# The last group's residual add, moved from VectorE into an accumulating scatter

## The chip, the cores and the metric

The kernel runs on one core of a Trainium2 chip. The metric is the device time of one execution in microseconds (us); several executions are timed and their median counts.

## What is computed

There are 2048 tokens of width 512 (x is 4 x 512 x 512). The first half adds to x the product of one of four experts, chosen by the token's id; an expert's gate, up and down weights are all the same 512 x 512 matrix, a slice of ctx. The second half adds a gated feed-forward product with 512 x 1536 weights that are rounded to eight-bit floats. Cut to what matters:

```python
x = x + tanh(g_xattn[0]) * experts(layernorm(x), token_ids, ctx)
gate = silu(layernorm(x) @ q(gate_w) * gate_scale)
up = layernorm(x) @ q(up_w) * up_scale
x = x + tanh(g_ffn[0]) * ((gate * up) @ q(down_w) * down_scale)
```

The last sum is the one that the change is about: x after the experts (x1 below), plus the scaled feed-forward product.

## The kernel before, in words

The tokens are sorted by expert. `order` holds, for each of 16 tiles of 128 sorted tokens, the row of x (and of the output) that each token has. GpSimd gathers the rows of x into `xs` (128 partitions, 16 tiles, 512 values) by an indirect DMA for each tile (L427). Nineteen expert steps (16 tiles and 3 places where a tile has two experts, `STEPS`) then add the expert's product into `xs` on VectorE (`add_expert`, L936, semaphore `x1_done`). After the last of them `xs` holds x1. Beside the steps GpSimd rounds the 36 weight slabs (`round_slab`, L481 and L484), and goes on with the late ones when the steps are over.

The feed-forward half goes over 4 groups of 4 tiles (`GROUPS`, `TPG`). For each group TensorE works through 12 units of the inner dimension: gate and up products (L1322), then the down product of a unit (`down_tile`, L1329), accumulated for the group's four tiles in the PSUM banks `ACC`. When a tile's accumulation ends, VectorE multiplies it by `dsb` (the down scale times tanh of g_ffn) into `slab_tile(g, t)`, which lies in the place of the group's transposed input `X2`, no longer needed, and signals `acc_free` (L1139). 

Who adds this to x1 depends on the group. For groups 0 to 2 GpSimd does: it waits for `acc_free`, adds into `xs` (L525), waits for its own `added`, and scatters the tile's rows to the output by an indirect DMA (L531). For group 3, the last, VectorE itself adds, right after the tile's scaling (L1142, semaphore `added_last`), and GpSimd only issues the scatter. GpSimd executes its queue in the order written: weight rounding, then tiles 0 to 15, then a wait for all 16 scatters (`stored`), after which the kernel ends.

TensorE's order at the very end is written out by hand: for tiles 0 to 2 of the last group the accumulations end first, each with its own signal, then comes the whole rest of tile 3 (its last three units, six matmuls).

Of the kernel before, what the change touches and what calls it, by code (L numbers as in the profile page):

```python
# [17 lines left out]
ALU = mybir.AluOpType  # L18
# [15 lines left out]
def build(nc, x, token_ids, ctx, g_xattn, g_ffn, gate_w, up_w, down_w, gate_scale, up_scale, down_scale, out):  # L34
    B, S, D = x.shape
    TOK = B * S
    TILES = TOK // P
# [4 lines left out]
    STEPS = TILES + E - 1  # L42
    GROUPS = TOK // 512
    TPG = TILES // GROUPS
# [12 lines left out]
    out_rows = out.rearrange("b s d -> (b s) d")  # L57
# [6 lines left out]
    with ExitStack() as stack:  # L64
        def sb(name, shape, dt):
            return stack.enter_context(nc.sbuf_tensor(name, shape, dt))

        def sem(name):
            return stack.enter_context(nc.semaphore(name))


        xs = sb("xs", [P, TILES, D], F32)
# [54 lines left out]
        order = sb("order", [P, TILES], I32)  # L127
# [114 lines left out]
        x1_done = sem("x1_done")  # L242
# [25 lines left out]
        acc_done = sem("acc_done")  # L268
        acc_free = sem("acc_free")
        added = sem("added")  # L270
        added_last = sem("added_last")
        stored = sem("stored")

        N_CONSTS = 14
# [1 line left out]
        def slab_tile(g, t):  # L276

            v = X2[:, g, :, :, :, :] if isinstance(g, int) else X2[:, ds(g, 1), :, :, :, :]
            pat = "p a k t i -> p (a k t i)" if isinstance(g, int) else "p g a k t i -> p (g a k t i)"
            return v.rearrange(pat).bitcast(F32)[:, t * D:(t + 1) * D]  # L280
# [112 lines left out]
        def _(pool):  # L393
            g = nc.gpsimd
# [124 lines left out]
                round_slab(n, slab_slot(n))  # L519


            for t in range(TILES):
                if t < TILES - TPG:
                    pool.wait_ge(acc_free, TPG + t + 1)
                    g.tensor_tensor(xs[:, t, :], xs[:, t, :], slab_tile(t // TPG, t % TPG),  # L525
                                    ALU.add).then_inc(added, 1)
                    pool.wait_ge(added, t + 1)
                else:

                    pool.wait_ge(added_last, t - (TILES - TPG) + 1)  # L530
                g.indirect_dma_start(out=out_rows[:], out_offset=bass.IndirectOffsetOnAxis(  # L531
                    ap=order[:, t:t + 1], axis=0), in_=xs[:, t, :], in_offset=None).then_inc(stored, 16)
            pool.wait_ge(stored, 16 * TILES)


# [207 lines left out]
        def _(dve):  # L743
            v = nc.vector
# [196 lines left out]
            def ffn_norms(norms, a0, a1):  # L941

                if a0 == 0:
                    dve.wait_ge(scales_done, 1)
                    dve.wait_ge(norm_done, EARLY_NORMS)
                    v.tensor_copy(late_norms[:, 0:2 * KC], SMALL[:, 4 * KC * KC:4 * KC * KC + 2 * KC])
                for a in range(a0, a1):

                    src = norms[:, (a - a0) * 2 * KC * KC:(a - a0 + 1) * 2 * KC * KC]
                    ins = v.tensor_reduce(col_ssq[:, :, a * KC:(a + 1) * KC],  # L950
                                          src.rearrange("p (w k j) -> p w j k", w=2, k=KC), AX.X, ALU.add)
                link(ins, norms_read, nread)
                c = slice(a0 * KC, a1 * KC)
                v.tensor_tensor(nn[:, c], col_ssq[:, 0, c], col_ssq[:, 1, c], ALU.mult)
                link(v.tensor_tensor(gu[:, c], gs[:, c], us[:, c], ALU.mult), fchain, fcount)
                link(v.tensor_tensor(gu2[:, c], gu[:, c], gu[:, c], ALU.mult), fchain, fcount)
                link(v.tensor_tensor(b2[:, c], nn[:, c], gu2[:, c], ALU.mult), fchain, fcount)
                v.tensor_scalar(b2c[:, c], b2[:, c], 1e-30, 1e38, ALU.max, ALU.min).then_inc(b2_done, 1)

            def ffn_scales(i, a0, a1):  # L960

                c = slice(a0 * KC, a1 * KC)
                dve.wait_ge(binv_done, i + 1)
                link(v.tensor_scalar(f_scale[:, c].bitcast(I32), f_top[:, c].bitcast(I32), POW2_MASK, None,
                                     ALU.bitwise_and), fchain, fcount)
                v.tensor_scalar(gate_mul[:, c], gs[:, c], 1.0 / X_SCALE, None, ALU.mult)
                link(v.tensor_scalar(up_mul0[:, c], us[:, c], 1.0 / X_SCALE, None, ALU.mult), fchain, fcount)
                v.tensor_tensor(up_mul[:, c], up_mul0[:, c], f_scale[:, c], ALU.mult)
                v.reciprocal(f_inv[:, c], f_scale[:, c]).then_inc(fscale_done, 1)
# [98 lines left out]
            last = v.value_load(walk_last[0:1, 0:1], min_val=0, max_val=4095)  # L1068
# [6 lines left out]
            def late_slabs(c):  # L1075

                for n in range(EARLY + 2 * c, min(EARLY + 2 * c + 2, SLABS)):
                    slab_big(n, slab_slot(n))

            def late_norm(c):  # L1080

                dve.wait_ge(norm_done, EARLY_NORMS + 2 * (c - 4))
                v.tensor_copy(late_norms[:, 2 * KC * (c - 4):2 * KC * (c - 3)],
                              GATE[(c + 1) % 2][:, 0:2 * KC]).then_inc(norm_read, 1)

            def unit_fuse(g, c):
                u = g * IC + c
                dve.wait_ge(up_done, u + 1)
                dve.wait_ge(sg_done, u + 1)
                if not (isinstance(g, int) and g * IC + c < 2):  # L1090
                    dve.wait_ge(fl_done, u - 1)
                v.scalar_tensor_tensor(out=fuse[:, c % 2, :], in0=UP[c % 2][:], scalar=up_mul[:, c:c + 1],  # L1092
                                       in1=sg[:, c % 2, :], op0=ALU.mult, op1=ALU.mult).then_inc(fuse_done, 1)

            def unit_low(g, c):
                u = g * IC + c
                if not (isinstance(g, int) and g * IC + c < 2 or is_last_unit(g, c)):
                    dve.wait_ge(down_done, u - 1)
                dve.wait_ge(fh_done, u + 1)  # L1099
                v.tensor_tensor(fuse_part(g, c, 1), fuse[:, c % 2, :], fuse_part(g, c, 0),  # L1100
                                ALU.subtract).then_inc(fl_done, 1)
# [16 lines left out]
            def group(g, first, last):  # L1118
                for c in range(2, IC):
                    unit_fuse(g, c)  # L1120
                    if first and 5 <= c < 8:
                        late_norm(c)
                    unit_low(g, c)
                    if first:
                        late_slabs(c)
                    if first and c == 7:
                        dve.wait_ge(norm_read, 3)
                        ffn_norms(late_norms, 2, 3)
                        ffn_scales(1, 2, 3)
                if not last:  # L1130
                    unit_fuse(g + 1, 0)
                    unit_low(g + 1, 0)

                for t in range(TPG):
                    if t < TPG - 1 or last:
                        dve.wait_ge(acc_done, g * (TPG - 1) + t + 1)
                    else:
                        dve.wait_ge(down_done, g * IC + IC)
                    v.tensor_tensor(slab_tile(g, t), ACC[t][:], dsb[:], ALU.mult).then_inc(acc_free, 1)  # L1139
                    if last:  # L1140
                        dve.wait_ge(acc_free, TPG + g * TPG + t + 1)
                        v.tensor_tensor(xs[:, g * TPG + t, :], xs[:, g * TPG + t, :], slab_tile(g, t),  # L1142
                                        ALU.add).then_inc(added_last, 1)
                if not last:
                    unit_fuse(g + 1, 1)
                    unit_low(g + 1, 1)

            group(0, True, False)
            with dve.Fori(1, GROUPS - 1) as gi:
                group(gi, False, False)  # L1150
            group(GROUPS - 1, False, True)


# [259 lines left out]
```

## Time and profile before

| | |
|---|---|
| Time, median of 3 runs | 439.34 us (437.16 to 439.57) |
| Profiled execution, its own time | 434.8 us |
| Its span, first to last instruction | 433.1 us |
| Busy: TensorE | 394.0 us |
| Busy: VectorE | 230.8 us |
| Busy: ScalarE | 188.7 us |
| Busy: GpSimd | 172.1 us |
| Scatter issue (L531), median of 16 | 983 ns |

In the rows below the engines are PE (TensorE matmuls), PEld (TensorE weight loads), DVE (VectorE), ACT (ScalarE), POOL (GpSimd) and SP (the queue that loads). A row of a timeline gives the start and the duration in us, engine, line, operation, what is written <- what is read, and in brackets how long the engine had been idle and who ended that. The program's names stand without their buffer numbers, so X is X2. A row of busy times gives the stretch and its length, the busy time (and number of instructions) of PE, PEld, DVE, ACT and POOL, the granted TensorE clock as a share of full speed, the busy share of the 16 DMA engines, and GB/s. An indirect DMA's row on POOL is the issue alone; its data moves later, and its landing is when its semaphore is complete.

### The profile page before, as it was taken

Reading aid. Unit: us, or ns where it says so; the run is one execution under the profiler, and the core shown is the slowest. Engines: PE = TensorE matmul, PEld = TensorE weight load, DVE = VectorE, ACT = ScalarE, POOL = GpSimd, SP = SyncE. Lnnn points to the kernel's source line nnn. Section 1 sums busy time; section 2 is a strip of 40 time slices with the busy share of each in tenths; the row PEclk is TensorE's granted clock in tenths of the full one; section 3 lists DMA queues with packets and bytes.
Section 4 is the critical chain, followed back from the end, with each engine's and each line's share of the span. In section 5 each row is a group of like instructions: output and inputs, shape, how many; then the busy total and the mean of one; then the engine's idle time right before and its main releaser. Section 6 shows DMA issues by size and latency. Waiting matters only on the chain. (4 is left out here: it accounts for less than half of the span.)

```text
span 433.1 us, 6969 instructions
## 1 busy us (share of the span) xinstructions
PE 394.0 (91%) x2012; PEld 197.4 (46%) x2013; DVE 230.8 (53%) x479; ACT 188.7 (44%) x305; POOL 172.1 (40%) x209
## 2 busy tenths in 40 slices
PE   3288989899989999899989999999999999999991
PEld 3245545465546555344434444444444444444440
DVE  5668888777776679558642423223522224232234
ACT  4456656776776664765352222222222222222220
POOL 3445489635595547789640520000800001700003
PEclk9769999999999999899999999999999999999996
DMA  6583411110122121222000110000100000200002
GB/s 208 185 289 103 119 49 30 51 43 24 50 73 51 39 82 50 65 82 90 10 0 0 51 48 2 0 0 2 73 24 0 0 0 0 97 2 1 2 0 97
DMA packets 10507, 22.64 MB, mean 52 GB/s; under 512 B 1624, under 2 KB 1648, under 8 KB 10480
## 3 DMA queue, kind: packets, MB, share of 16 engines
q1 hardware_dynamic: 7920, 13.92, 10.7%
q0 software_dynamic: 2560, 8.39, 5.6%
q8 instruction: 13, 0.21, 0.2%
q14 instruction: 14, 0.11, 0.1%
HBM read 18.11 MB, written 4.19 MB: 51 GB/s over the span
## 5 line engine op out<-in xcount | busy, mean ns | idle before, releaser
L1322 PE MATMUL bank<-X,W 128*128 128x512 f16 (+1 forms) x768 | 174.6, 381 | 0.0
L1322 PEld LDWEIGHTS bank<-X,W 128*128 128x128 bf16 x768 | 75.5, 98 | 90.8 <-issue 1.6
L1092 DVE SCALAR_TENSOR_TENSOR cs<-bank,up_mul,cs 128x512 f32<-128x512 f32 x48 | 36.0, 750 | 112.7 <-PE bank L1322 107.2
L1329 PE MATMUL bank<-W,cs 128*128 128x512 bf16 x376 | 88.7, 379 | 2.0 <-DVE cs L1100 2.0
L681 ACT ACTIVATE cs<-bank,gate_mul 128x512 f32<-128x512 f32 x48 | 32.9, 686 | 81.7 <-PE bank L1322 79.3
L525 POOL TENSOR_TENSOR xs<-xs,X 128x512 f32<-128x512 f32 x12 | 15.3, 1273 | 123.9 <-DVE X L1139 123.7
L688 ACT ACTIVATE cs<-cs 128x512 f16<-128x512 f32 x47 | 29.5, 628 | 76.5 <-DVE cs L1092 75.5
L1329 PEld LDWEIGHTS bank<-W,cs 128*128 128x128 f16 x376 | 36.5, 98 | 45.9 <-DVE cs L1100 2.5
L1100 DVE TENSOR_TENSOR cs<-cs 128x512 f16<-128x512 f32 x47 | 34.5, 734 | 36.8 <-ACT cs L688 34.4
L481 POOL TENSOR_TENSOR w_sum<-ws,w_big 128x512 f32<-128x512 f32 x36 | 47.2, 1311 | 5.5 <-DVE w_big L887 3.5
L484 POOL TENSOR_TENSOR W<-w_sum,w_big 128x512 bf16<-128x512 f32 (+1 forms) x36 | 46.4, 1290 | 3.4 <-POOL w_sum L481 1.1
L531 POOL DMA_INDIRECT out<-xs,order x16 | 16.7, 1045 | 50.9 <-DVE xs L1142 47.5
L435 POOL TENSOR_TENSOR ln_tab<-prep,ln_half 128x1 f32<-128x1 f32 (+2 forms) x25 | 16.7, 668 | 46.9 <-DVE prep L785 46.7
L1230 PE MATMUL bank<-Mh,xTh 128*128 x76 | 29.8, 393 | 2.7 <-DVE xTl L907 1.6
L1230 PE MATMUL bank<-Ml,xTh 128*128 x76 | 29.8, 392 | 0.0
L1230 PE MATMUL bank<-Mh,xTl 128*128 x76 | 29.6, 390 | 0.0
L1230 PE MATMUL bank<-Mh,hTh 128*128 x76 | 28.8, 379 | 0.0
L1230 PE MATMUL bank<-Ml,hTh 128*128 x76 | 28.8, 379 | 0.0
L1230 PE MATMUL bank<-Mh,hTl 128*128 x76 | 28.8, 379 | 0.0
L887 DVE TENSOR_SCALAR w_big<-w_big 128x512 f32<-128x512 f32 x36 | 25.7, 738 | 1.5 <-ACT w_big L585 1.4
L585 ACT ACTIVATE w_big<-ws 128x512 f32<-128x512 f32 x36 | 21.3, 618 | 6.3 <-DMA ws<-in_L_ffn_up_w 3.4
L1183 PE MATMUL bank<-ident,cs 128*128 128x128 f32 x64 | 10.7, 323 | 11.3 <-DVE Ml L881 8.5
(148 smaller groups left out, 430.4 us busy)
## 6 DMA issues: line engine op xcount, KB each, us to landing
cs<-in_ctx SPq DMA_DIRECT2D x4, 1024.0 KB, 5.6
ws<-in_L_ffn_gate_w SPq DMA_DIRECT2D x12, 256.0 KB, 2.6
ws<-in_L_ffn_up_w SPq DMA_DIRECT2D x12, 256.0 KB, 2.6
ws<-in_L_ffn_down_w SPq DMA_DIRECT2D x12, 256.0 KB, 2.6
dsc<-in_L_ffn_down_scale SPq DMA_DIRECT2D x1, 256.0 KB
xs<-in_x,order POOLq DMA_INDIRECT x16, 3.7
out<-xs,order POOLq DMA_INDIRECT x16, 2.8
ids<-in_itok_BxS SPq DMA_DIRECT2D x1, 8.0 KB, 1.6
```

Source lines behind the costliest of these rows:

```text
L435: g.tensor_tensor(ln_tab[:, rr, lo:hi, 0], prep[:, slot:slot + 1, lo:hi, 1], ln_half[:, :, lo:hi], ALU.pow).then_inc(ln_chain, 1)
L481: g.tensor_tensor(w_sum[:], ws[:, slot], w_big[:, slot], ALU.add).then_inc(sum_done, 1)
L484: g.tensor_tensor(dst, w_sum[:], w_big[:, slot], ALU.subtract).then_inc(q_done, 1)
L585: a.activation(w_big[:, slot], ws[:, slot], ACT.Abs, scale=FP8_STEP).then_inc(abs_done, 1)
L681: a.activation(sg[:, c % 2, :], GATE[c % 2][:], ACT.Silu, scale=gate_mul[:, c:c + 1]).then_inc(sg_done, 1)
L688: a.activation(fuse_part(g, c, 0), fuse[:, c % 2, :], ACT.Copy).then_inc(fh_done, 1)
L887: v.tensor_scalar(w_big[:, slot], w_big[:, slot], FP8_FLOOR, None, ALU.max).then_inc(big_done, 1)
L1092: v.scalar_tensor_tensor(out=fuse[:, c % 2, :], in0=UP[c % 2][:], scalar=up_mul[:, c:c + 1], in1=sg[:, c % 2, :], op0=ALU.mult, op1=ALU.mu ...
L1100: v.tensor_tensor(fuse_part(g, c, 1), fuse[:, c % 2, :], fuse_part(g, c, 0), ALU.subtract).then_inc(fl_done, 1)
L1230: ins = t_.matmul(dst[:], lhs[:, k * P:(k + 1) * P], rhs, start=(n == 0), stop=(n == 3 * KC - 1))
L1322: ins = t_.matmul(dst[c % 2][:], w, x2_group(g, part, k), start=(k == 0 and part == 0), stop=(k == KC - 1 and part == 1))
L1329: ins = t_.matmul(ACC[t][:], fuse_part(g, c, part)[:, t * P:(t + 1) * P], W8[:, down_slab(c), :], start=(c == 0 and part == 0), stop=(c == ...
```

## The change

The last group's tiles (12 to 15) are written to the output twice. First, as soon as all expert steps are done and GpSimd has finished rounding weights, plain scatters write their x1 rows (semaphore `stored_x1`). At the end, VectorE only scales; GpSimd waits for `acc_free` and issues a scatter of the scaled product itself, with an addition to what lies in the output rows (`compute_op=ALU.add`). Ahead of these stands a wait until the first four scatters have landed. Groups 0 to 2 are as before.

```diff
@@ -519,17 +519,23 @@
-            for t in range(TILES):
-                if t < TILES - TPG:
-                    pool.wait_ge(acc_free, TPG + t + 1)
-                    g.tensor_tensor(xs[:, t, :], xs[:, t, :], slab_tile(t // TPG, t % TPG),
-                                    ALU.add).then_inc(added, 1)
-                    pool.wait_ge(added, t + 1)
-                else:
-
-                    pool.wait_ge(added_last, t - (TILES - TPG) + 1)
+            def scatter(t, rows, op, done):
                 g.indirect_dma_start(out=out_rows[:], out_offset=bass.IndirectOffsetOnAxis(
-                    ap=order[:, t:t + 1], axis=0), in_=xs[:, t, :], in_offset=None).then_inc(stored, 16)
+                    ap=order[:, t:t + 1], axis=0), in_=rows, in_offset=None, compute_op=op).then_inc(done, 16)
+
+            pool.wait_ge(x1_done, STEPS)
+            for t in range(TILES - TPG, TILES):
+                scatter(t, xs[:, t, :], ALU.bypass, stored_x1)
+            for t in range(TILES - TPG):
+                pool.wait_ge(acc_free, TPG + t + 1)
+                g.tensor_tensor(xs[:, t, :], xs[:, t, :], slab_tile(t // TPG, t % TPG),
+                                ALU.add).then_inc(added, 1)
+                pool.wait_ge(added, t + 1)
+                scatter(t, xs[:, t, :], ALU.bypass, stored)
+            pool.wait_ge(stored_x1, 16 * TPG)
+            for t in range(TILES - TPG, TILES):
+                pool.wait_ge(acc_free, TPG + t + 1)
+                scatter(t, slab_tile(t // TPG, t % TPG), ALU.add, stored)
             pool.wait_ge(stored, 16 * TILES)
@@ -1137,10 +1143,6 @@
                     v.tensor_tensor(slab_tile(g, t), ACC[t][:], dsb[:], ALU.mult).then_inc(acc_free, 1)
-                    if last:
-                        dve.wait_ge(acc_free, TPG + g * TPG + t + 1)
-                        v.tensor_tensor(xs[:, g * TPG + t, :], xs[:, g * TPG + t, :], slab_tile(g, t),
-                                        ALU.add).then_inc(added_last, 1)
```

## Rows read from the trace of the kernel before

**Rows 1.** The page, busy us (share of the span) of each engine.

```profile
PE 394.0 (91%) x2012; PEld 197.4 (46%) x2013; DVE 230.8 (53%) x479; ACT 188.7 (44%) x305; POOL 172.1 (40%) x209
```

**Rows 2.** The chain of waits, its end: start us, us, what.

```profile
418.51 3.04 PE bank L1329 x14
421.54 0.02 issue
421.57 0.70 DVE X L1139
422.29 0.69 DVE xs L1142
...
426.27 0.70 DVE xs L1142
426.98 0.27 issue
427.24 0.96 POOL out L531
```

**Rows 3.** Timeline of the end, VectorE, TensorE and GpSimd.

```profile
421.57 0.69 DVE L1139 TENSOR_TENSOR X<-bank,dsb 128x512 f32<-128x512 f32 x1 [0.88 <-PE bank L1329]
...
423.09 0.59 PE L1329 MATMUL bank<-W,w_sum 128*128 128x512 bf16 x2
423.26 0.96 POOL L531 DMA_INDIRECT out<-xs,order  x1 [46.43 <-DVE xs L1142]
...
424.59 0.96 POOL L531 DMA_INDIRECT out<-xs,order  x1 [0.37 <-DVE xs L1142]
...
427.24 0.96 POOL L531 DMA_INDIRECT out<-xs,order  x1 [0.37 <-DVE xs L1142]
```

**Rows 4.** Busy time by quarter microsecond, from 428.50 on.

```profile
428.50:428.75 0.25, 0.00 (x0) 0.00 (x0) 0.00 (x0) 0.00 (x0) 0.00 (x0) 0.50 0.00 0
428.75:429.00 0.25, 0.00 (x0) 0.00 (x0) 0.00 (x0) 0.00 (x0) 0.00 (x0) 0.50 0.96 377
429.00:429.25 0.25, 0.00 (x0) 0.00 (x0) 0.00 (x0) 0.00 (x0) 0.00 (x0) 0.50 0.98 377
429.25:429.50 0.25, 0.00 (x0) 0.00 (x0) 0.00 (x0) 0.00 (x0) 0.00 (x0) 0.50 0.77 295
429.50:429.75 0.25, 0.00 (x0) 0.00 (x0) 0.00 (x0) 0.00 (x0) 0.00 (x0) 0.50 0.02 0
```

**Rows 5.** Scatters (L531): ns min/median/max of the issue; last issue's landing.

```profile
L531 POOL DMA_INDIRECT out<-xs,order x16: 958/983/1153, 243.4 to 427.2; - x16
...
DMA to landing us min/median/max: 2.7/2.7/2.7
```

**Rows 6.** Timeline of VectorE, the last expert step's addition.

```profile
172.65 0.73 DVE L936 SCALAR_TENSOR_TENSOR xs<-bank,y_scale,xs 128x512 f32 x1
```

**Rows 7.** Timeline of GpSimd around its idle time from 221 us.

```profile
220.11 1.27 POOL L484 TENSOR_TENSOR W<-w_sum,w_big 128x512 bf16<-128x512 f32 x1
241.86 1.27 POOL L525 TENSOR_TENSOR xs<-xs,X 128x512 f32<-128x512 f32 x1 [20.49 <-DVE X L1139]
```

**Rows 8.** Busy time in two stretches of 5 us.

```profile
220.00:225.00 5.00, 3.01 (x15) 1.23 (x14) 2.19 (x3) 3.29 (x6) 1.30 (x2) 1.00 0.00 0
225.00:230.00 5.00, 5.00 (x25) 2.29 (x24) 1.45 (x3) 1.92 (x3) 0.00 (x0) 1.00 0.00 0
```

**Rows 9.** Timeline of GpSimd, two of the gathers issued back to back.

```profile
43.89 0.94 POOL L427 DMA_INDIRECT xs<-in_x,order  x1 [0.30 <-issue]
45.14 0.95 POOL L427 DMA_INDIRECT xs<-in_x,order  x1 [0.31 <-issue]
```

**Rows 10.** The page's DMA issues: gathers, then scatters, us to landing.

```profile
xs<-in_x,order POOLq DMA_INDIRECT x16, 3.7
out<-xs,order POOLq DMA_INDIRECT x16, 2.8
```

More of the change, by code:

```diff
@@ L270, in build @@
         added = sem("added")
-        added_last = sem("added_last")
+        stored_x1 = sem("stored_x1")
         stored = sem("stored")
```

## The prediction

> **What bounds the kernel now.** I read the page's busy shares first, then the end of the chain of waits, then the last 12 us in order of time, then the DMA share in quarter microseconds. The first view says that TensorE sets the span: it is busy for 394.0 of 433.1 us, and VectorE and GpSimd for about half of it or less [rows 1]. The change touches TensorE nowhere, so at most the stretch after TensorE's last needed result can move. The chain shows that stretch: TensorE is on it until 421.54; from 421.57 VectorE alternates a scaling and an addition four times, until 426.97; then comes one scatter issue on GpSimd from 427.24 [rows 2]. So the chain's tail is eight VectorE operations of 0.69 us and one issue. The timeline shows what the chain doesn't name: GpSimd issues all four scatters of the last group in that stretch, 0.96 us each, starting at 423.26, 424.59, 425.92 (this one not shown) and 427.24, that is 1.33 us apart, each 0.3 to 0.4 us after its addition; TensorE's very last matmuls end at 423.68 [rows 3]. GpSimd is therefore nearly as full as VectorE here, which matters below. The windows show what follows an issue: for the last one (427.24) the DMA engines are idle until 428.75, work at 0.96 to 0.98 share until 429.5, and are done [rows 4]. Its landing is 2.7 us after the issue [rows 5], at 429.94. The span ends 3.16 us later, with nothing busy; the change leaves that end as it is.
>
> I write the landing of a scatter as: issue start + 1.5 us to the first data, 0.7 us of burst (0.96 + 0.98 + 0.77 of a quarter microsecond each is 0.68), 0.5 us to the semaphore.
>
> **Part 1: the early scatters of x.** Four more indirect scatters go on GpSimd's queue, behind the last weight rounding and ahead of the first addition of group 0, with a wait on the last expert step. The wait costs nothing: the last addition of an expert's product into xs is at 172.65 [rows 6], and GpSimd only comes free at 220.11 + 1.27 = 221.38 [rows 7]. The four issues take 4 x 1.25 = 5.0 us (the spacing comes from the row in part 2), until about 226.4. What is queued behind them is the addition of tile 0, which before started at 241.86 after 20.49 us of idling [rows 7]; so they lie in idle time with 15 us to spare. Without that cover they would move group 0's additions and scatters by up to 5.0 us, and even that would reach no other engine: only GpSimd's own scatters follow from these additions. The transfers (1 MB more written) find an empty DMA side: 0 GB/s from 220 to 230 [rows 8]. No queue of SP or ACT is passed. The second new wait, for these four scatters to have landed, stands ahead of the last group's scatters; with issue by 226 and landing 3 us on it has been met for some 190 us. Cost: 0.
>
> **Part 2: VectorE's additions go, GpSimd gets the chain.** The four additions (0.69 us each, 2.8 us) leave VectorE. Its first scaling still ends at 422.26. The second and third follow at once and end at 422.95 and 423.65; the fourth waits for TensorE's end at 423.68 and ends near 424.4. That is 2.6 us earlier than the 426.97 of before. But it isn't the gain, because the issues now stand end to end. The first can start 0.28 us after the first scaling, at 422.54. The nearest row for back-to-back indirect issues is the row of gathers, one after another with no wait between: 43.89, 45.14, so 1.25 us apart (0.94 busy and 0.31 of issue) [rows 9]. The fourth then starts at 422.54 + 3 x 1.25 = 426.29 instead of 427.24. All four scalings are ready before their issue (424.4 + 0.28 against 426.29), so GpSimd alone sets the pace, and 0.95 us is all that can be saved if an accumulating scatter costs what a plain one costs. Nothing excludes this end of the range, but nothing goes below it: the accumulating form does all the plain one does.
>
> **Part 3: the price of accumulating.** No row of before shows an accumulating transfer. It has two prices.
>
> The burst b. A plain burst keeps the 16 engines at a share of 0.96 to 0.98 for its whole length [rows 4], so it is limited by the engines' work, not by latency. The accumulating one must read the rows of the product and the rows in the output, and write the output. Lower end: 0.7 us, if the second read is free. If the reads are what fills the engines, it is twice that, 1.4 us, and this I take, because the row shows no idle share in which a second read would fit. Upper end: a burst that is bound by going to memory and back for each row. The nearest row is the gather, whose landing of 3.7 us against 2.8 shows that reading memory first costs 0.9 us more for one transfer [rows 10]; if every one of the two halves of a burst doubled and then waited about that long again, b would be near 2.8 us (an estimate: 1.4 + 0.9 + 0.5). The Trainium skill, page "Collectives: The Full Stack", section on why ReduceScatter is half of AllGather, says that an adding transfer emits two read descriptors per chunk on the same read ring, so that it moves data at half the rate of a copy. No row of before shows this, and it speaks against the change; by it b is 1.4 us, against 0.7 us for a free second read, and the landing is 0.7 us later than without it.
>
> The issue i. GpSimd works out the transfer's addresses in this instruction. Lower end 0.95 us. Upper end twice that, 1.9 us, if a second source doubles the work. The plain scatter itself varies from 0.958 to 1.153 us [rows 5]. I take 1.2 us, just above its slowest row, since most of the instruction (one row of indices read, 128 rows of one operand) stays. With 0.3 us between, the spacing p is 1.5 us.
>
> **The sum.** With b below p the last landing is 422.54 + 3p (fourth start), + 1.5 to first data, + (p - 1.25) for the longer issue, + b, + 0.5: together 423.29 + 4p + b. Plain prices: 423.29 + 5.0 + 0.7 = 428.99, 0.95 us earlier than 429.94. My values: 423.29 + 6.0 + 1.4 = 430.69, 0.75 us later. Issue at its upper end (p = 2.2): 433.49, 3.55 us later. So the 2.6 us that VectorE gives back are taken by GpSimd's spacing, and the rest by the accumulating form. The profiled execution took 434.8 us, 4.5 below the median of the runs (439.34) and 2.4 below the fastest of them; on its own base the forecast is 435.55, and carried to the median it is 440.1. A measurement of this kernel can tell about 0.5%, here 2.2 us, from no change.
>
> **Rivals.**
> (a) The accumulating form is about free: 0 to 0.95 us faster, 438.4 at best. For it: the issue handles the same 128 rows, and the two reads may overlap. Against: the full DMA share in a burst. This is still no measurable change.
> (b) Slower, on the other side: the burst becomes the bound. Its place is the DMA queue after 424, with four transfers one behind another. With b above p the landing is 423.29 + p + 4b; at p = 1.25 it passes 2.2 us over before once b exceeds 1.9 us, 2.7 times the plain burst. At b = 2.8 it is 435.74, 5.8 us later: 445.1. For it: each row is read, added and written in memory, and the gather's longer landing. Against: bursts of 377 GB/s show that 16 engines have many rows in flight.
> (c) Slower, through the issue: with b = 1.4 it decides from p = 1.86, an issue of 1.56 us; at 1.9 us it gives 442.9. For it: two sources per row to write out. Against: nothing in the trace.
> (d) Faster by over 2.2 us: if VectorE's whole 2.6 us came through, 436.7. That needs the fourth issue to follow its scaling at 424.7; three issues of 0.95 us stand between 422.54 and there, which don't fit. What is left of this case is the unevenness of the runs: three of the same kernel lie between 437.16 and 439.57.
>
> **How the numbers follow.** The forecast case (0 to 2.2 us slower) gets 0.48, (a) 0.22, (b) 0.13, (c) 0.11, (d) 0.06. No measurable change is the first two: 0.70. Slower is (b) and (c): 0.24. Faster is (d): 0.06. Range: the best price gives 438.4; a median can fall about 1.2 us lower, half the spread of the runs shown, so 437.2. Up: (c) at its upper end, 442.9, so 443.0; the far part of (b) is left out.
>
> **What would show it.** Step by step in the profile after: four extra scatters near 221.4 to 226.4 with the addition of tile 0 still at about 241.9; at the end four VectorE scalings and no addition, the last ending near 424.4; the first accumulating issue at about 422.5 and the others spaced p = 1.5 us by their own length, not by waits for VectorE; DMA bursts of 1.4 us per transfer at a full share; last landing near 430.7. I am wrong if the issue takes over 1.56 us, if a burst takes over 1.9 us, if DMA share between the bursts is low while a transfer is under way (latency, not work), or if anything before 421 us moves.

## Result and profile after

The changed kernel takes 440.85 us (median of 9 runs, 438.83 to 443.51); the kernel before, on the same chip, 436.41 us (9 runs, 434.94 to 439.57). The ratio is 1.0096, with a 95% interval from 1.0063 to 1.0129: about 4.2 us slower. The time lies in the range given. But this is slower by more than 0.5%, which had 0.24; the most likely case, no measurable change, had 0.70.

That 440.85 us lies near the forecast of 440.1 is luck. The forecast put 0.75 us on a kernel before of 439.34 us, the median of three runs; over nine runs that kernel is at 436.41. So the base was 2.9 us too high and the change 3.4 to 3.7 us too small. On the forecast's own base, 439.34 + 4.2 = 443.5 us would lie above its upper end of 443.0.

The profiled execution has a span of 439.4 us against 433.1, a difference of 6.3 us. Not all of it belongs to the change. GpSimd's timeline of after, where it ends the weight rounding and meets the early scatters:

```profile
221.25 1.27 POOL L484 TENSOR_TENSOR W<-w_sum,w_big 128x512 bf16<-128x512 f32 x1
222.69 1.10 POOL L523 DMA_INDIRECT out<-xs,order  x1 [0.18 <-issue]
224.09 1.07 POOL L523 DMA_INDIRECT out<-xs,order  x1 [0.30 <-issue]
225.47 0.96 POOL L523 DMA_INDIRECT out<-xs,order  x1 [0.30 <-issue]
226.73 0.96 POOL L523 DMA_INDIRECT out<-xs,order  x1 [0.30 <-issue]
243.01 1.27 POOL L531 TENSOR_TENSOR xs<-xs,X 128x512 f32<-128x512 f32 x1 [15.33 <-DVE X L1145]
```

The last rounding starts at 221.25 instead of 220.11, tile 0's addition at 243.01 instead of 241.86 [rows 7]. So this execution was already 1.14 us late before the first instruction that the change adds. Of two single executions that says nothing; it only means that the rest has to be read from a common mark. I take the start of the last group's first scaling: 421.57 before [rows 3], 422.71 after, again 1.14 us later. Between the two marks nothing moved. The last 17 us of after, from the timeline:

```profile
423.32 1.28 DVE L1145 TENSOR_TENSOR X<-bank,dsb 128x512 f32<-128x512 f32 x2
...
424.19 1.62 POOL L523 DMA_INDIRECT out<-X,order  x1 [46.22 <-DVE X L1145]
...
424.87 0.69 DVE L1145 TENSOR_TENSOR X<-bank,dsb 128x512 f32<-128x512 f32 x1 [0.27 <-PE bank L1331]
426.11 1.59 POOL L523 DMA_INDIRECT out<-X,order  x1 [0.30 <-issue]
428.00 1.55 POOL L523 DMA_INDIRECT out<-X,order  x1 [0.30 <-issue]
429.86 1.55 POOL L523 DMA_INDIRECT out<-X,order  x1 [0.30 <-issue]
```

The four scalings are done at 425.56, 2.85 us after the first one's start; forecast were 2.83. GpSimd is what goes on: 1.55 to 1.62 us an issue instead of 0.96 [rows 3], 1.86 to 1.92 us apart, and spaced by "issue", no longer by VectorE. The landings of the first, then of the third and fourth, and the DMA side in half microseconds (last two columns: share of the 16 engines, GB/s):

```profile
DMA to landing us min/median/max: 4.8/4.8/4.8
...
DMA to landing us min/median/max: 5.6/5.8/6.1
```

```profile
426.50:427.00 0.50, 0.00 (x0) 0.00 (x0) 0.00 (x0) 0.00 (x0) 0.50 (x1) 1.00 0.63 61
427.00:427.50 0.50, 0.00 (x0) 0.00 (x0) 0.00 (x0) 0.00 (x0) 0.50 (x1) 1.00 1.00 127
...
432.00:432.50 0.50, 0.00 (x0) 0.00 (x0) 0.00 (x0) 0.00 (x0) 0.00 (x0) 0.50 1.09 160
432.50:433.00 0.50, 0.00 (x0) 0.00 (x0) 0.00 (x0) 0.00 (x0) 0.00 (x0) 0.50 1.06 102
...
435.00:435.50 0.50, 0.00 (x0) 0.00 (x0) 0.00 (x0) 0.00 (x0) 0.00 (x0) 0.50 0.10 16
```

Before, a burst of 0.7 us at 377 GB/s was followed by a pause [rows 4]. Now the engines are busy without a pause from 426.3 to about 435, at 57 to 168 GB/s. The last landing is at 429.86 + 6.1 = 435.96 (the answer's last figure; the 5.6 is the third transfer's), 13.25 us after the first scaling's start, against 429.94 - 421.57 = 8.37 before. That is 4.9 us, near the 4.2 that timing gives.

One more stretch differs, behind the last landing. There the kernel's close has a DRAIN on GpSimd's sequencer (L64, the line that opens the kernel's scope), here before, then after:

```profile
L64 POOLq DRAIN  x1: 2693/2693/2693, 430.2 to 430.2; - x1
```

```profile
L64 POOLq DRAIN  x1: 3015/3015/3015, 436.1 to 436.1; - x1
```

It takes 3.02 us (3015 ns) instead of 2.69. With this the spans are accounted for: 1.14 us before the mark, 4.9 to the last landing and 0.3 behind it are 6.3 us.

### The profile page after: what moved, and what is told of

The parts are those of the page before. It is cut to its first block and busy times, and to the rows that moved or that the text cites. A ratio compares the mean times of both kernels' runs of the same rounds, so it can differ in the third digit from the quotient of the medians.

```text
span 439.4 us, 6949 instructions
## 1 busy us (share of the span) xinstructions
PE 395.1 (90%) x1991; PEld 198.6 (45%) x2013; DVE 226.2 (51%) x475; ACT 188.4 (43%) x305; POOL 178.4 (41%) x213
## 3 DMA queue, kind: packets, MB, share of 16 engines
q0 software_dynamic: 3136, 9.44, 7.5%
HBM read 18.11 MB, written 5.24 MB: 53 GB/s over the span
## 5 line engine op out<-in xcount | busy, mean ns | idle before, releaser
L1331 PE MATMUL bank<-W,cs 128*128 128x512 bf16 x355 | 86.3, 379 | 3.1 <-DVE cs L1106 2.0
L531 POOL TENSOR_TENSOR xs<-xs,X 128x512 f32<-128x512 f32 x12 | 15.2, 1267 | 118.9 <-DVE X L1145 118.6
L1106 DVE TENSOR_TENSOR cs<-cs 128x512 f16<-128x512 f32 x47 | 35.6, 757 | 36.5 <-ACT cs L694 34.5
L523 POOL DMA_INDIRECT out<-X,order x4 | 6.3, 1579 | 47.1 <-DVE X L1145 46.2
L893 DVE TENSOR_SCALAR w_big<-w_big 128x512 f32<-128x512 f32 x36 | 23.7, 683 | 1.6 <-ACT w_big L591 1.6
L1185 PE MATMUL bank<-ident,cs 128*128 128x128 f32 x64 | 12.1, 351 | 10.6 <-DVE Ml L887 7.8
```

The costliest lines, as they stand in the source:

```text
L893: v.tensor_scalar(w_big[:, slot], w_big[:, slot], FP8_FLOOR, None, ALU.max).then_inc(big_done, 1)
L1331: ins = t_.matmul(ACC[t][:], fuse_part(g, c, part)[:, t * P:(t + 1) * P], W8[:, down_slab(c), :], start=(c == 0 and part == 0), stop=(c == ...
```

## Experiments

Each kernel was timed against the kernel before on the same chip, and its tail read from its own profile: T is the time from the first scaling's start to the last landing, 8.37 us before and 13.25 after. T is read from one execution of each kernel.

### 1. Plain scatters in the new order

```diff
-                scatter(t, slab_tile(t // TPG, t % TPG), ALU.add, stored)
+                scatter(t, slab_tile(t // TPG, t % TPG), ALU.bypass, stored)
```

> The changed kernel with its last four scatters plain instead of accumulating (the output rows of the last group get the feed-forward product alone; x1 is left out there). Theory A, the loss is the accumulating form alone: issues 0.96 us long and 1.25 apart, bursts of 0.7 us at full DMA share, last landing 0.95 us nearer to the first scaling than in the kernel before (7.4 us after its start instead of 8.4), so 0 to 1 us faster than before, ratio 0.998. Rival B, the new order on GpSimd costs by itself (the first issue came 0.80 us after its scaling in the changed kernel, 0.28 before): the first issue is late here too, the rest as in A, ratio 0.999 to 1.000. Rival C, the early scatters or the missing additions cost something elsewhere: ratio over 1.003.

Ratio 1.0012 (0.9984 to 1.0041). Its timeline:

```profile
420.15 1.89 DVE L1145 TENSOR_TENSOR X<-bank,dsb 128x512 f32<-128x512 f32 x3 [0.88 <-PE bank L1331]
421.62 0.96 POOL L523 DMA_INDIRECT out<-X,order  x1 [46.21 <-DVE X L1145]
...
422.88 0.96 POOL L523 DMA_INDIRECT out<-X,order  x1 [0.30 <-issue]
424.15 0.96 POOL L523 DMA_INDIRECT out<-X,order  x1 [0.30 <-issue]
425.42 0.96 POOL L523 DMA_INDIRECT out<-X,order  x1 [0.30 <-issue]
```

Issues are 0.96 us again and 1.27 apart, and each lands after 2.7 us: T = 425.42 + 2.7 - 420.15 = 7.97. So the accumulating form accounts for 5.3 of T, and the new order by itself is 0.4 us shorter than before, not 0.95. The half microsecond between is in the first line: the first scaling ends at 420.84, and the issue starts at 421.62, 0.78 us later, where before it was 0.28 [rows 3]. That was rival B's reading. The timing's interval holds B's 0.999 to 1.000 and C's "over 1.003" and ends 0.0004 above A's 0.998, so it decides little.

### 2. Only the early scatters, with their wait

```diff
+            pool.wait_ge(x1_done, STEPS)
+            for t in range(TILES - TPG, TILES):
+                g.indirect_dma_start(out=out_rows[:], out_offset=bass.IndirectOffsetOnAxis(
+                    ap=order[:, t:t + 1], axis=0), in_=xs[:, t, :], in_offset=None).then_inc(stored_x1, 16)
             for t in range(TILES):
+                if t == TILES - TPG:
+                    pool.wait_ge(stored_x1, 16 * TPG)
...
+                        dve.wait_ge(stored_x1, 16 * TPG)
                         v.tensor_tensor(xs[:, g * TPG + t, :], xs[:, g * TPG + t, :], slab_tile(g, t),
```

> The kernel before with only the four early scatters of x1 added (the last group is written twice, both times plainly). Theory A, they lie in GpSimd's idle time: ratio 1.000, the addition of tile 0 starts about as long after the last weight rounding as in the kernel before. Rival C, they are part of the loss, through 1 MB more of traffic or GpSimd's queue: ratio over 1.003.

Ratio 1.0034 (1.0004 to 1.0064), which is rival C's figure. Its timeline shows another cause:

```profile
421.31 0.69 DVE L1150 TENSOR_TENSOR xs<-xs,X 128x512 f32<-128x512 f32 x1
...
422.64 0.69 DVE L1150 TENSOR_TENSOR xs<-xs,X 128x512 f32<-128x512 f32 x1
422.78 1.38 POOL L538 DMA_INDIRECT out<-xs,order  x1 [46.93 <-DVE xs L1150]
...
424.47 1.02 POOL L538 DMA_INDIRECT out<-xs,order  x1 [0.30 <-issue]
```

The first addition ends at 422.00, the issue starts 0.78 us later, and this plain issue takes 1.38 us instead of 0.96. The two go with different things.

The longer issue goes with VectorE. The late start puts the issue into VectorE's second addition (422.64 to 423.33), where the issue of before, at 423.26, started between two additions. Over all kernels here, the ten issues of the last group that start while such an addition runs are longer than usual, by what is left of the addition less about 0.13 us: with 0.55 us left 0.42 longer (experiments 2, 3 and 6), with 0.54 left 0.41 (experiment 4), with 0.45 left 0.35 (experiment 7), with 0.16 to 0.19 left 0.03 to 0.06. An issue that starts before the addition is not longer, though the addition runs beside it. After and experiment 1 have no addition there, and their first issue is late and not longer. This is read from the traces alone; no run was made to test it.

The late start goes with the wait; experiment 5 takes it up. VectorE's addition in this kernel waits for two semaphores too, and starts 0.72 us after its scaling's start, as before.

GpSimd is then behind VectorE for all four, and the last issue comes 0.86 us later than before (427.12 - 420.59 = 6.53 against 5.67). T = 9.23. With the longer DRAIN at the close that is 1.2 us, and the ratio is 1.5: no cost of the early scatters ahead of the last group shows here.

### 3. Only the last tile accumulated

In experiments 3, 4, 6 and 7 the tiles that are not accumulated are added on VectorE as before, and only the accumulated ones are scattered early.

```diff
+                if t in [15]:
+                    pool.wait_ge(acc_free, TPG + t + 1)
+                    scatter(t, slab_tile(t // TPG, t % TPG), ALU.add, stored)
+                else:
+                    pool.wait_ge(added_last, sum(u not in [15] for u in range(TILES - TPG, t + 1)))
+                    scatter(t, xs[:, t, :], ALU.bypass, stored)
```

> Only the last tile (15) is scattered early and accumulated; tiles 12 to 14 are added on VectorE as before. Shows one accumulating transfer that nothing of its kind stands in front of. Theory A1, an accumulating transfer by itself takes 2.3 us of burst and its issue 1.57 us: last issue 5.6 us after the first scaling's start (GpSimd's pace), landing 4.9 us later, at 10.5 against 8.4 before: 2.1 us slower, ratio 1.005. Rival A2, the long bursts of the changed kernel come only from four of them in flight together, one alone takes 0.7 to 1.4 us: landing 3.3 to 4.0 us after the issue, 0.5 to 1.2 us slower, ratio 1.001 to 1.003.

Ratio 1.0081 (1.0049 to 1.0112). The accumulating issue (427.84, 1.62 us long) lands 4.9 us later, T = 11.37, 3.0 us more than before: 2.2 for the transfer's longer landing, 0.8 for the issue, which came at 6.47 instead of 5.67, behind a first issue that was late and long as in experiment 2. The transfer in quarter microseconds:

```profile
429.75:430.00 0.25, 0.00 (x0) 0.00 (x0) 0.00 (x0) 0.00 (x0) 0.00 (x0) 0.50 0.00 0
430.00:430.25 0.25, 0.00 (x0) 0.00 (x0) 0.00 (x0) 0.00 (x0) 0.00 (x0) 0.50 1.72 131
430.25:430.50 0.25, 0.00 (x0) 0.00 (x0) 0.00 (x0) 0.00 (x0) 0.00 (x0) 0.50 1.16 90
430.50:430.75 0.25, 0.00 (x0) 0.00 (x0) 0.00 (x0) 0.00 (x0) 0.00 (x0) 0.50 0.77 82
430.75:431.00 0.25, 0.00 (x0) 0.00 (x0) 0.00 (x0) 0.00 (x0) 0.00 (x0) 0.50 0.92 131
431.00:431.25 0.25, 0.00 (x0) 0.00 (x0) 0.00 (x0) 0.00 (x0) 0.00 (x0) 0.50 0.81 139
431.25:431.50 0.25, 0.00 (x0) 0.00 (x0) 0.00 (x0) 0.00 (x0) 0.00 (x0) 0.50 0.98 180
431.50:431.75 0.25, 0.00 (x0) 0.00 (x0) 0.00 (x0) 0.00 (x0) 0.00 (x0) 0.50 1.09 197
431.75:432.00 0.25, 0.00 (x0) 0.00 (x0) 0.00 (x0) 0.00 (x0) 0.00 (x0) 0.50 0.40 66
432.00:432.25 0.25, 0.00 (x0) 0.00 (x0) 0.00 (x0) 0.00 (x0) 0.00 (x0) 0.50 0.20 33
```

One accumulating transfer with nothing in front of it keeps the engines at work for 2.2 us. The shares of these rows sum to 8.05 quarters (single ones read over 1, so this is rough), 2.0 us of work of all 16 engines, against 0.68 for a plain one: three times as much. A2 (one alone takes 0.7 to 1.4 us) falls.

### 4. Only the first tile accumulated

The same edit with `[12]` for `[15]`.

> Only the first tile of the last group (12) is scattered early and accumulated; tiles 13 to 15 are added on VectorE and scattered plainly. Theory A1: its long issue and burst lie under the other tiles' work; its issue starts 0.97 us after the first scaling's start, the others follow at 2.8, 4.1 and 5.35, last landing 8.05 against 8.4: 0.3 us faster, which timing can't tell from 1.000. Rival A3, an accumulating transfer holds back what is behind it in the queue: the plain ones land 1 us or more later than their issue plus 2.7, ratio over 1.002.

Ratio 1.0036 (1.0007 to 1.0065). The first issue starts 0.78 us after its scaling and takes 2.03 us, 0.41 longer than the first of after: it starts in VectorE's addition, as in experiment 2. The plain ones behind it land after 3.7, 3.0 and 2.7 us: the first two are held back by the long burst, the last no more, so A3 holds for a while and does not reach the end. T = 427.47 + 2.7 - 421.10 = 9.07, 0.7 us more than before, all of it from the late issues (the last starts 6.37 us after the first scaling's start, before 5.67).

### 5. The wait moved away from the last group

What after and the first four have in common is a first issue behind two waits, one met long before (`stored_x1`) and one that ends now. Their traces have something there that the kernel before lacks, an instruction of GpSimd's sequencer at the line of the wait that ends now. In after that is `pool.wait_ge(acc_free, ...)`, L537:

```profile
L537 POOLq EVENT_SEMAPHORE  x1: 17/17/17, 423.4 to 423.4; - x1
```

It runs 0.04 us after the scaling's end, and the DMA starts 0.73 us behind it.

```diff
             for t in range(TILES - TPG):
+                if t == 2 * TPG:
+                    pool.wait_ge(stored_x1, 16 * TPG)
                 pool.wait_ge(acc_free, TPG + t + 1)
...
-            pool.wait_ge(stored_x1, 16 * TPG)
             for t in range(TILES - TPG, TILES):
```

> The changed kernel with the wait for the early scatters (stored_x1) moved from the last group's first issue to the addition of tile 8, some 50 us earlier. In all kernels of the first four runs that had this wait, the last group's first issue came 0.8 us after what it waited for, against 0.28 in the kernel before, and in three of them it was also 0.4 us longer. Theory D: two waits on one DMA instruction cause it. Then the first issue comes 0.28 us after its scaling and the last landing is 0.5 us nearer to the first scaling's start (12.8 us instead of 13.3); ratio about 1.009. Rival E: it is the first issue after 46 us of idling in a kernel with a longer program, or the early scatters do it in another way: 0.8 us stays.

Ratio 1.0103 (1.0073 to 1.0133), which can't be told from the 1.0096 of after. Its timeline:

```profile
421.37 1.89 DVE L1146 TENSOR_TENSOR X<-bank,dsb 128x512 f32<-128x512 f32 x3 [0.88 <-PE bank L1332]
...
422.34 1.62 POOL L523 DMA_INDIRECT out<-X,order  x1 [45.34 <-DVE X L1146]
```

The first issue starts 0.28 us after its scaling (422.06). The last is at 428.01 and lands after 5.5: T = 12.14, 1.1 us less than after and 0.7 less than the 12.8 expected. So theory D is right about the place; timing isn't fine enough to show the gain. That it is two waits as such isn't separated from the order of the two or from the kind of semaphore (`stored_x1` is counted up by DMAs). The moved wait has a price where it now stands: the addition of tile 8 comes 0.36 us later after its scaling than before (0.07 in experiments 7 and 9), which reaches nothing that the end hangs on.

### 6. Half the bytes, the same rows

This is the kernel of experiment 3 with half rows in its accumulating scatter. `order2` is twice `order`, worked out at the start; `out_halves` is the output with rows of 256 values.

```diff
-                    scatter(t, slab_tile(t // TPG, t % TPG), ALU.add, stored)
+                    g.indirect_dma_start(out=out_halves[:], out_offset=bass.IndirectOffsetOnAxis(
+                        ap=order2[:, t:t + 1], axis=0), in_=slab_tile(t // TPG, t % TPG)[:, 0:256],
+                        in_offset=None, compute_op=ALU.add).then_inc(stored, 16)
```

> The kernel with the last tile alone accumulated, with its accumulating scatter over the first half of each row (256 of 512 values, 128 rows as before; the second half of those output rows keeps x1). There the whole-row transfer kept the DMA engines at work for 2.2 us and landed 4.9 us after its issue, the issue took 1.62 us. Theory F, the burst is limited by bytes: 1.1 us, landing 3.8 us after the issue. Rival G, by the number of rows: the burst stays 2 us or more and the landing 4.7 to 4.9. The issue stays about 1.6 us in both, since it has 128 rows to write out.

Ratio 1.0041 (1.0018 to 1.0065). The issue takes 1.62 us, as for whole rows; the landing 3.8 us. The DMA engines of this kernel work from 428.5 to 429.75:

```profile
428.50:428.75 0.25, 0.00 (x0) 0.00 (x0) 0.00 (x0) 0.00 (x0) 0.00 (x0) 0.50 0.81 49
428.75:429.00 0.25, 0.00 (x0) 0.00 (x0) 0.00 (x0) 0.00 (x0) 0.00 (x0) 0.50 0.84 86
429.00:429.25 0.25, 0.00 (x0) 0.00 (x0) 0.00 (x0) 0.00 (x0) 0.00 (x0) 0.50 1.02 119
429.25:429.50 0.25, 0.00 (x0) 0.00 (x0) 0.00 (x0) 0.00 (x0) 0.00 (x0) 0.50 1.11 172
429.50:429.75 0.25, 0.00 (x0) 0.00 (x0) 0.00 (x0) 0.00 (x0) 0.00 (x0) 0.50 0.61 90
```

Theory F: half the bytes, half the burst. The queue's packets, experiment 3, then 6:

```profile
q0 software_dynamic: 2704, 8.65, 6.0%
```

```profile
q0 software_dynamic: 2704, 8.52, 5.8%
```

Both move the same number of packets. So the burst goes with bytes, and not with the number of rows or packets; the issue does not go with bytes.

### 7. First tile accumulated, wait moved

The edits of 4 and 5 together.

> The kernel with only the first tile of the last group accumulated, with the wait for the early scatter moved to the addition of tile 8. Theory D: first issue 0.28 us after its scaling and 1.6 us long instead of 0.78 and 2.03; last issue 5.4 us after the first scaling's start (before: 5.67), landing 8.1 (before: 8.37): 0.3 us faster than the kernel before, ratio 0.999, which timing can't tell from 1. Rival E: as without the move, last issue 6.4 after the first scaling's start, ratio 1.002 to 1.003.

Ratio 1.0002 (0.9975 to 1.0029). The first issue is 0.28 us late and 1.62 long, as D says. But the plain issue behind it took 1.31 us instead of 0.96, so the last came at 5.80, not 5.4, and T = 8.50. That issue again starts in an addition of VectorE, with 0.45 us of it left:

```profile
423.18 0.69 DVE L1154 TENSOR_TENSOR xs<-xs,X 128x512 f32<-128x512 f32 x1
423.42 1.31 POOL L524 DMA_INDIRECT out<-xs,order  x1 [0.30 <-issue]
```

This was the version meant to beat both kernels; it equals the kernel before.

### 8. Only the early scatters, wait moved

The edits of 2 and 5 together.

> The kernel before with the four early scatters added and the wait for them moved to the addition of tile 8 on GpSimd. With the wait at the last group it measured 1.0034. Theory D: the loss was the wait's 0.9 us at the end (0.5 late and 0.4 longer), so the last issue is back at 5.67 us after the first scaling's start and the ratio at 1.000 to 1.001. Rival C: the four early scatters themselves cost something before the end: the tail is as in the kernel before, and the ratio stays over 1.002.

Ratio 1.0015 (0.9988 to 1.0042). The end is that of the kernel before again:

```profile
423.44 0.96 POOL L538 DMA_INDIRECT out<-xs,order  x1 [46.06 <-DVE xs L1150]
...
427.42 0.96 POOL L538 DMA_INDIRECT out<-xs,order  x1 [0.36 <-DVE xs L1150]
```

The last issue is 427.42 - 421.74 = 5.68 us after the first scaling's start, before 5.67. What differs from experiment 2 is where GpSimd's wait stands, so theory D holds for plain scatters too. The interval holds both D's 1.000 and rival C's 1.002.

### 9. Four accumulating scatters of half rows

The edits of 5 and 6, for all four tiles.

> The changed kernel with the early wait, and with all four accumulating scatters over the first half of each row (the second half of those rows keeps x1). Issues stay 1.6 us long and 1.87 apart, the burst of each is 1.1 us and so shorter than the spacing. Theory H, with whole rows the bursts queue (2.2 to 2.3 us each against a spacing of 1.87) and set the end: here the queue is gone and the last landing is at 0.97 + 3 x 1.87 + 3.8 = 10.4 us after the first scaling's start, against 12.1 with whole rows and 8.4 in the kernel before; each transfer lands 3.8 us after its issue, ratio 1.005. Rival I, each transfer's own latency sets the landing and four in flight slow one another whatever their size: landings over 4.5 us after the issue, last landing over 11.2, ratio over 1.007.

Ratio 1.0061 (1.0040 to 1.0083). Landings 3.9, 3.7, 3.8 and 3.9 us after their issues, T = 428.32 + 3.9 - 421.68 = 10.54. Theory H: the DMA engines pause between the bursts (no data from 426.25 to 426.50, for one), nothing queues, and GpSimd's spacing sets the pace. With whole rows T was 12.14, so the bytes cost 1.6 us of the end and the longer issues and the rest 2.2.

### 10. Plain scatters, wait moved

The edits of 1 and 5.

> The changed kernel with the early wait and with plain instead of accumulating scatters at the end (the last group's rows get the product alone, x1 is left out there). It is what the new order could give at best. Theory A with D: first issue 0.28 us after its scaling, spacing 1.27, last landing 0.97 + 3 x 1.27 + 2.7 = 7.5 us after the first scaling's start against 8.4: 0.9 us faster than the kernel before, ratio 0.998. Rival C, something ahead of the end costs too (the two kernels with early scatters and no late price measured 1.0015 and 1.0012): ratio 1.000 or above although the tail is 0.9 us shorter.

Ratio 0.9992 (0.9963 to 1.0021); T = 426.65 + 2.7 - 421.88 = 7.47, 0.9 us less than before. That is the ceiling of this order of work with free accumulation, and the timing does not tell it from nothing. The expectation counts experiment 1 among the kernels without a late price; it had the late first issue.

## Why the prediction was right or wrong

**What bounds the kernel, parts 1 and 2: right, but for the kernel's close.** The work that both kernels have between the weight rounding and the last group kept its place. The early scatters lay in idle time, with 15.33 us left; GpSimd paces the end, VectorE's 2.6 us are lost to its spacing, and 0.95 us was the ceiling (0.9 in experiment 10). The four early issues took 5.17 us from the end of the rounding (222.52) to the end of the last (227.69) against 5.0, their starts 1.26 to 1.40 apart. The prediction says that each issue of before comes 0.3 to 0.4 us after its addition; it is 0.28, which is what its sum uses.

**"The change leaves that end as it is", and the early scatters at 0: wrong, by 0.3 us.** GpSimd's DRAIN at the close takes 2.69 us in the kernel before, 2.77 in the four kernels with one early scatter, and 3.02 in the seven with four: about 0.08 us for each indirect DMA more. No idle time covers that.

**The second new wait, "Cost: 0": wrong, by 0.5 us in after.** I asked only whether the wait would be met. It was, for some 190 us, but it stood ahead of the last group's first issue, beside another wait. Experiments 5 and 8 show that it delays that issue there and not when it stands 50 us earlier. T fell by 1.1 us in experiment 5, 0.6 more than the late start: the landings followed one another after 1.7, 2.1 and 2.4 us there, in after by 2.4, 2.2 and 2.4, which one execution of each can't settle.

**Part 3, the issue at 1.2 us: undersized.** It took 1.55 to 1.62, a spacing of 1.86 to 1.92 against my 1.5, just over the 1.86 from which rival (c) decides. I had taken the plain row's own spread as the measure; the accumulating form costs 0.6 us for 128 rows, also with half the bytes (experiment 6). Whether that is the second source or the larger number of packets (below) isn't separated.

**Part 3, the burst at 1.4 us: undersized.** It is 2.2 us alone and about 2.3 in a queue (landings at 429.0 and 435.96 in after, three transfers apart). That is over both the spacing and the 1.9 us from which rival (b) decides; 2.8 was its upper end. The argument that a full DMA share leaves no room for a second read fits the result, but counting reads gave a factor of 2, and the engines' work grew threefold. The second read itself is not seen: experiment 1 and after have the same 9.44 MB in this queue's row and the same 18.11 MB read from memory on their pages. The Trainium skill, page "Collectives: The Full Stack", section on why ReduceScatter is half of AllGather, gives, for the adding step of a collective, two read descriptors per chunk and half the rate of a copy; by that rule, too, the burst would have been 1.4 us. The measurement decides: here an accumulating scatter ran at a third of the rate. What the third part is stays open. The data is also cut finer. Experiment 1, then after, with the same number of indirect DMAs:

```profile
q0 software_dynamic: 2880, 9.44, 6.3%
```

```profile
q0 software_dynamic: 3136, 9.44, 7.5%
```

That is 64 packets more for each of the four, 144 instead of 80, for the same bytes. But the number of packets takes little of the time. Experiment 6 has 144 as well, with half the bytes, and its 16 engines work 1.1 us against 2.0: drawn through these two, the part that does not go with bytes is 0.2 us (an estimate), of the 1.3 that the accumulating form adds. The rest goes with bytes, and how it divides between reading, adding and writing is open.

**The formula.** For b above p it was 423.29 + p + 4b. With the measured sizes: 423.29 + 1.89 + 4 x 2.3 = 434.38, and 0.5 for the wait, 434.88, which is 4.94 us later than before's 429.94. Measured: 4.9. That is no independent test, since the 2.3 was read from the same landings. In experiment 5, without the 0.5, it gives T = 12.81 against 12.14: there the formula is 0.7 us too long, and with the lone transfer's 2.2 us still 0.3. So rivals (b) and (c) came together, and they add up less than singly, since of two stages in a row only the slower one counts four times: with bursts of 2.3 us, the longer issue adds only 0.6 us for the first data and nothing for the next three. Experiment 9, where bursts are short, pays the longer issue four times.

**What stays open.** Several kernels with early scatters measure some 0.5 us more than their T says: 1.0015 is 0.65 us in experiment 8, where T is unchanged, and 1.0012 is 0.5 us more in experiment 1, where T is 0.4 us less. The longer DRAIN is 0.3 us of that in both. Each interval also holds what T and the DRAIN say together, so a further small price of the early scatters is neither shown nor ruled out. Open too: why two waits delay an indirect DMA, why T is shorter in experiment 5 than the wait explains, and why the accumulating form triples the engines' work.

## What to carry to other kernels

An accumulating DMA is not a free addition: it costs the issuing engine and the DMA engines more than a plain one (1.6 us against 0.96, and 2.0 against 0.68 here), and at the end of a kernel, where each transfer is awaited, nothing covers that; 0.69 us of VectorE for each tile was the cheaper place. Before taking an operation off one engine of a two-engine chain, see how full the other one is: here GpSimd's 1.27 us spacing stood right behind VectorE's 1.33. And a wait that is long met still belongs away from an instruction that the end hangs on. Work put into idle time can come back at the close: four scatters issued some 200 us before the end made it 0.3 us longer.

## What was new about the hardware

- Two waits ahead of one indirect DMA instruction of GpSimd: it starts 0.78 to 0.79 us after the event instead of 0.28, in all six kernels that have it (after and experiments 1 to 4 and 6), with a separate EVENT_SEMAPHORE of 17 ns at the line of the second wait. In the five kernels with the wait moved the start is at 0.28 again. An addition of VectorE behind two waits (experiment 2) was not late; one of GpSimd's (tile 8, experiments 5 and 7 to 10) was by 0.07 to 0.36 us.
- An indirect DMA's issue on GpSimd that starts while VectorE adds two tiles in the core's own memory (`xs` and `X`) takes longer, by what is left of the addition less about 0.13 us: up to 0.42 us in ten issues. One that starts just before the addition (423.26 against 423.62 in the kernel before) takes its usual 0.96 us, and so do those that start in a scaling, which reads a PSUM bank, but for one of 0.99 us (experiment 4).
- An accumulating indirect scatter of 128 rows of 2 KB (f32): issue 1.55 to 1.62 us (plain 0.96), burst 2.2 us (0.7), landing 4.9 us (2.7), 16-engine work 2.0 us (0.68), 144 packets (80). With 1 KB rows: issue 1.62, burst 1.1, landing 3.8, 144 packets.
- A plain transfer right behind an accumulating one landed 3.7 to 3.8 us after its issue (experiments 4 and 7), 1.0 to 1.1 us later than usual.
- The DRAIN at the close: 2.69 us with 16 indirect scatters in the kernel, 2.77 with 17, 3.02 with 20.
